# Naming the gathered rows earlier: an edit in VectorE's and GpSimd's order of the expert stage

## The chip, the cores and the metric

The kernel runs on one core of one Trainium2 chip. The metric is the device time of one execution in microseconds (us). In the text PE is TensorE (matrix products and transposes), ACT is ScalarE, DVE is VectorE, POOL is GpSimd and SP is SyncE, which only issues transfers here. Each engine works through its own list of instructions in order. Engines meet through semaphores: an instruction adds to a counter when it has ended, and another engine's list holds at a wait until the counter has the value.

## The reference, cut to what matters

The input is 16 batches of 56 tokens of 512 values, and 16 contexts of 1500 rows of 512 values. A layer of cross attention comes first, then a layer with 16 experts, of which each token uses its best four, and one shared expert that all tokens use:

```python
x = x + xattn(layernorm(x), ctx, Wq, bq, Wk, bk)        # softmax(Q K^T / sqrt(512)) ctx
h = layernorm(x)
scores = sigmoid(h @ gate_w.T) + bias                   # 896 tokens x 16 experts
w, idx = top_k(scores, 4);  w = w / (sum(w) + 1e-20)
out = sum over the four experts e of  w_e * (silu(h Wg_e) * (h Wu_e)) Wd_e
out = out + (silu(h Sg) * (h Su)) Sd
x = x + out
```

## The kernel before, in words

**Stages.** Attention is done in eight turns of two batches, to about 280 us of the trace. The rest is the expert layer. Its tokens are worked in tiles of 128 rows. Tiles 0 to 6 are the 896 tokens in their order, for the shared expert. From tile 7 on (`SHARED` is 7) come the routed tiles: each belongs to one expert and holds up to 128 tokens that chose it. How many there are depends on the data; in this run there are 34, tiles 7 to 40. DVE writes a table (`plan`) that says for each tile which expert it has, which column of the token lists names its rows, how many thirds of the experts' weights have to be split by then, and which tile was the first of its expert. The engines read it into registers, in `entry`.

**One routed tile.** GpSimd fetches its 128 rows from HBM with an indirect DMA into `taken[i]` (`gather`, L439 to L446); the row numbers stand in `take_at[i]`. A row is the 512 normalised values and the token's 16 expert weights. PE turns the rows into columns (bank `b4`, `taken_transpose`), ACT rounds them into `taken_hi`, and DVE writes what the rounding left, `taken_lo` (`taken_to_lo`, L1295). PE then forms the two up products in twelve matrix instructions of 512 columns: high part of the rows by high and low part of the weights (`up_hi`, eight), low part of the rows by the high weights (`up_lo`, four). ACT takes a tanh (`half`), DVE makes from it `gated_rows` and then `z_rows`, into which the token's weight for this expert goes (`silu_rows`; the weight is `taken_w`, one column of the gathered row, copied by `take_weight`, L1307 to L1309). PE turns `z_rows` (`z_transpose`, bank `b5`), ACT rounds (`zt_hi`), DVE writes the rest (`zt_lo`, `z_to_lo`, L1311), and PE forms the down product in six instructions, the last two of which need `zt_lo` (`down`). ACT copies the result into `y_sb[i]` (`keep_y`, L925) and the place of its rows into `add_at[i]` (`name_add`, L930). GpSimd adds the tile into the output with an indirect DMA (`add`, L448 to L461).

**Buffers.** `taken`, `take_at`, `add_at`, `y_sb` and `taken_w` have two places each, which the tiles use in turn. `keep_y` of tile t waits until the add of tile t-2 has landed. An add also waits until all adds of the experts before its own have landed, since the same token's row can be in both.

**Weights.** Experts' weights come from HBM on SP's queue into three places of `w_raw`. ACT rounds them in thirds into `w_hi` (L896), DVE subtracts into `w_lo` (`third_lo`, L1279). Both do so at the end of a step, in `more_thirds`, as many thirds as the plan has due. ACT's part waits until PE has ended the down product before. SP loads a further expert when the thirds of an earlier one have been split.

**Order of a step.** The engines' lists are written out by hand; there is a loop over pairs of steps. In step t:

- PE: `z_transpose(t-1)`, `up_lo(t)`, transposes of tile t+1, `down(t-1)`, wait for the weights, `up_hi(t+1)`.
- ACT: `z_to_hi(t-1)`, `half(t)`, `taken_to_hi(t+1)`, `keep_y(t-2)`, `name_add(t-2)`, `more_thirds(t+1)`.
- DVE: `z_to_lo(t-1)`, `silu_rows(t)`, `taken_to_lo(t+1)`, `take_weight(t+1)`, `name_take(t+3)` (L1302 to L1305), `more_thirds(t+1)`.
- GpSimd, two tiles at a time: `gather(t+5)`, `add(t)`, in this order. The gather waits for `take_named`, which `name_take` of the same tile raises.

So GpSimd's gather of tile T waits for the end of DVE's step T-3, in which ACT also writes the result of tile T-5, whose add stands behind that gather. That the buffer of tile T-2 has been read before the gather overwrites it needs no wait of its own: DVE names tile T after `taken_to_lo(T-2)`, and that follows the transposes.

Of the kernel before, what the change touches and what calls it, by code (L numbers as in the profile page):

```python
# [37 lines left out]
SHARED = TOKENS // P  # L38
# [34 lines left out]
def moe_attention_kernel(nc, x, ctx, ctx_t, wq, bq, wk, bk, gate_t, gate_b, experts, shared,  # L73
# [14 lines left out]
    with es:  # L88
# [3 lines left out]
        def sem(name):  # L92
            return es.enter_context(nc.semaphore(name))
# [32 lines left out]
        with nc.sbuf_tensor("shared_raw", [P, WFREE], fp32) as shared_raw:  # L126
# [125 lines left out]
                              for n in ("b3", "b4", "b5", "b6", "b7"))  # L252
# [24 lines left out]
        gathered, added, shared_taken = ([sem(f"{n}{i}") for i in range(2)] for n in ("gathered", "added", "shared_taken"))  # L277
        take_named, add_named = sem("take_named"), sem("add_named")
        tt_ready, taken_hi_ready, taken_lo_ready, w_ready = (sem(n) for n in ("tt_ready", "taken_hi_ready",
                                                                              "taken_lo_ready", "w_ready"))  # L280
        gu_ready, half_ready, gated_ready, z_rows_ready = (sem(n) for n in ("gu_ready", "half_ready", "gated_ready",
                                                                           "z_rows_ready"))
# [10 lines left out]
        def settle(eng):  # L293
            eng.sem_inc(waited, 1)
# [26 lines left out]
        def entry(eng, table, at, most):  # L321

            return eng.value_load(plan[0:1, bass.ds(at + table, 1)], min_val=0, max_val=most)  # L323

        def inner_pairs(eng):

            return eng.value_load(plan[0:1, T_HALF:T_HALF + 1], min_val=TOKENS * TOPK // P // 2 - 2, max_val=TILES // 2 - 2)
# [81 lines left out]
        @block.gpsimd  # L409
        def _(pool):  # L410
            nc.gpsimd.memset(neg_half[:], -0.5).then_inc(pool_step, 1)
            nc.gpsimd.memset(zero_rows[:], 0.0).then_inc(init_ready, 1)
            pool.wait_ge(pool_step, 1)

            pool.wait_ge(init_ready, 1)

            for i in range(2):
                pool.dma_start(out[TOKENS + i * HALF:TOKENS + (i + 1) * HALF, :], zero_rows[0:HALF, 0:DIM]
                               ).then_inc(added[i], 16)

            def power(i):
                pool.wait_ge(var_ready, i + 1)
                nc.gpsimd.tensor_tensor(rstd[:], var_eps[:], neg_half[:], ALU.pow).then_inc(rstd_ready, 1)  # L423

            power(0)
            power(1)
            with pool.Fori(1, PAIRS - 1) as p:
                power(p * 2)
                power(p * 2 + 1)
            power(2 * PAIRS - 2)  # L430

            def add_shared(t):

                pool.wait_ge(ysb_ready, t + 1)
                nc.gpsimd.indirect_dma_start(
                    out[:, :], bass.IndirectOffsetOnAxis(ap=shared_at[:, t:t + 1], axis=0),
                    y_sb[:, t % 2 * DIM:(t % 2 + 1) * DIM], None, compute_op=ALU.add).then_inc(added[t % 2], 16)


            def gather(t, i):  # L440

                pool.wait_ge(take_named, t - (SHARED - 1))
                settle(pool)
                nc.gpsimd.indirect_dma_start(  # L444
                    taken[i][:, :], None, h_rows[:, :], bass.IndirectOffsetOnAxis(ap=take_at[i][:, 0:1], axis=0)
                    ).then_inc(gathered[i], 16)  # L446

            def add(t, i):  # L448

                first = entry(pool, T_FIRST, t - SHARED, TILES + SHARED)  # L450
                pool.wait_ge(added[0], pool.snap((first + 1) // 2 * 16 + 16, min_val=16, max_val=16 * TILES))
                settle(pool)
                pool.wait_ge(added[1], pool.snap(first // 2 * 16 + 16, min_val=16, max_val=16 * TILES))
                settle(pool)
                pool.wait_ge(add_named, t - (SHARED - 2))
                settle(pool)
                pool.wait_ge(ysb_ready, t + 1)
                settle(pool)
                nc.gpsimd.indirect_dma_start(  # L459
                    out[:, :], bass.IndirectOffsetOnAxis(ap=add_at[i][:, 0:1], axis=0), y_sb[:, i * DIM:(i + 1) * DIM],  # L460
                    None, compute_op=ALU.add).then_inc(added[i], 16)  # L461

            pool.wait_ge(shared_named, 1)
            power(2 * PAIRS - 1)
            pool.wait_ge(acc_stored, 2 * 32)
            add_shared(0)
            add_shared(1)
            add_shared(2)
            add_shared(3)
            pool.wait_ge(init_stored, 16)  # L470
            pool.wait_ge(h_stored, PAIRS * 32 + 16)
            pool.wait_ge(plan_ready, 1)
            n_inner = inner_pairs(pool)
            gather(SHARED, 1)
            gather(SHARED + 1, 0)
            add_shared(4)
            gather(SHARED + 2, 1)
            gather(SHARED + 3, 0)
            add_shared(5)
            gather(SHARED + 4, 1)  # L480
            add_shared(6)
            with pool.Fori(0, n_inner - 1) as pair:
                for k in range(2):
                    t = pair * 2 + (SHARED + k)
                    gather(t + 5, k)
                    add(t, 1 - k)
            t = n_inner * 2 + (SHARED - 2)
            gather(t + 5, 0)
            for k in range(6):
                add(t + k, 1 - k % 2)  # L490
            for i in range(2):
                pool.wait_ge(added[i], n_inner * 16 + 48 + (SHARED + 1 - i) // 2 * 16)
# [519 lines left out]
        def _(dve):  # L1012
# [272 lines left out]
            def more_thirds(t):  # L1285

                upto_t = entry(dve, T_PIECES, t - SHARED, THIRDS * EXPERTS)
                with dve.If_lt(done, upto_t):
                    with dve.Fori(dve.snap(done, min_val=0, max_val=THIRDS * EXPERTS), upto_t) as n:
                        dve.wait_ge(hi_ready, n + 1)  # L1290
                        settle(dve)
                        third_lo(dve.snap(n % (SETS * THIRDS) * THIRD, min_val=0, max_val=(SETS * THIRDS - 1) * THIRD))
                    dve.reg_mov(done, upto_t)

            def taken_to_lo(t):  # L1295
                dve.wait_ge(taken_hi_ready, t + 1)
                settle(dve)
                nc.vector.tensor_tensor(taken_lo[:].rearrange("p k n -> p (k n)"), b4[:, :],  # L1298
                                        taken_hi[:].rearrange("p k n -> p (k n)"), ALU.subtract
                                        ).then_inc(taken_lo_ready, 1)  # L1300

            def name_take(t, i):  # L1302

                col = entry(dve, T_COL, t - SHARED, LISTS + EXPERTS - 1)
                nc.vector.tensor_copy(take_at[i][:], list_at[:, bass.ds(col, 1)]).then_inc(take_named, 1)  # L1305

            def take_weight(t, i):  # L1307
                e = entry(dve, T_EXPERT, t - SHARED, EXPERTS - 1)
                nc.vector.tensor_copy(taken_w[:, i:i + 1], taken[i][:, bass.ds(e + DIM, 1)]).then_inc(w_ready, 1)  # L1309

            def z_to_lo(t):  # L1311
                dve.wait_ge(zt_hi_ready, t + 1)
                settle(dve)
                nc.vector.tensor_tensor(zt_lo_cols[:], b5[:, 0:INNER], zt_hi_cols[:], ALU.subtract  # L1314
                                        ).then_inc(zt_lo_ready, 1)

            def silu_rows(t, i):
                gate_rows(t, i)
                dve.wait_ge(w_ready, t - (SHARED - 1))
                settle(dve)  # L1320
                dve.wait_ge(gated_ready, t + 1)
                settle(dve)
                nc.vector.scalar_tensor_tensor(z_rows[:], gated_rows[:], taken_w[:, i:i + 1], tile_banks[i][:, INNER:], ALU.mult,
                                               ALU.mult).then_inc(z_rows_ready, 1)
# [58 lines left out]
            dve.wait_ge(hi_ready, THIRDS)  # L1383
            third_lo(2 * THIRD)
            n_inner = inner_pairs(dve)
            taken_to_lo(SHARED)
            take_weight(SHARED, 1)
            name_take(SHARED + 2, 1)

            def step(t, i):  # L1390
                z_to_lo(t - 1)
                silu_rows(t, i)
                taken_to_lo(t + 1)
                take_weight(t + 1, 1 - i)
                name_take(t + 3, 1 - i)
                more_thirds(t + 1)

            more_thirds(SHARED)
            step(SHARED, 1)
            with dve.Fori(0, n_inner + 1) as pair:  # L1400
                for k in range(2):
                    step(pair * 2 + (SHARED + 1 + k), k)
            t = n_inner * 2 + (SHARED + 3)
# [67 lines left out]
```

## Time and profile before

| what | us |
|---|---|
| median of 3 runs | 553.05 (546.88 to 556.69) |
| the profiled execution | 548.86 |
| span of its trace | 547.1 |
| attention, from the start | about 280 |
| first routed step to last product of PE | about 321 to 531 |
| PE, DVE, ACT, POOL busy | 490.3, 259.4, 155.4, 110.8 |

The profiled execution's own time is 1.8 us above its span and 4.2 us below the median of the runs. The page's rows have an engine, a line of the kernel, what is written and read, how often, the busy time and the idle time ahead of it with what ended it. "issue" as such a cause means that the engine's sequencer was busy with its own registers and branches, or that the trace shows no other cause. PE's clock stands in tenths or as a share of full speed.

### The profile page before, as it was taken

The page shows a single profiled execution, that of the slowest core. Times are in us where ns is not written, and L with a number is a line of the kernel's source. Part 1 is how long each engine was busy: PE and PEld are TensorE (multiplying, and loading weights), DVE is VectorE, ACT ScalarE, POOL GpSimd, SP SyncE. Part 2 cuts the span into 40 slices and gives each one's busy share as a digit, 9 for nine tenths or more (in the row PEclk, how much of TensorE's full clock was granted, in tenths as well). Part 3 has the DMA queues.
Part 4 walks back from the last instruction along what each step waited for, and adds up shares of the span by engine and source line. Part 5 has one row for each costly group of instructions (what it writes and reads, how often), then busy time and mean ns, then how long its engine had stood idle before and what let it go on. Part 6 is the DMA issues. An engine that isn't in the chain of part 4 may idle for free.

```text
span 547.1 us, 10804 instructions
## 1 busy us (share of the span) xinstructions
PE 490.3 (90%) x2472; PEld 293.8 (54%) x2473; DVE 259.4 (47%) x707; ACT 155.4 (28%) x303; POOL 110.8 (20%) x100
## 2 busy tenths in 40 slices
PE   3999999999999999999899878989898988899970
PEld 1583535353636363543467646767676656577740
DVE  3203337373645445453448874545455646545420
ACT  0000402020203021210222263435363545444430
POOL 1000000000000000000002233444344442444431
PEclk9969999999999999999799989999898999899985
DMA  9999999999999999999646667876749585455552
GB/s 214 399 423 424 388 424 419 411 428 401 427 400 425 400 423 411 417 426 418 241 114 159 157 207 197 270 230 115 195 124 261 98 212 174 80 84 108 97 64 32
DMA packets 28231, 149.04 MB, mean 272 GB/s; under 512 B 4072, under 2 KB 4200, under 8 KB 16424
## 3 DMA queue, kind: packets, MB, share of 16 engines
q1 hardware_dynamic: 15832, 123.08, 56.6%
q0 software_dynamic: 8720, 20.21, 20.2%
q10 hardware_dynamic: 3664, 5.57, 3.3%
q8 instruction: 7, 0.11, 0.1%
q14 instruction: 8, 0.07, 0.0%
HBM read 133.84 MB, written 15.01 MB: 272 GB/s over the span
## 4 chain that ended last, share of the span: by engine, by line
PE 67%; DMA 14%; issue 6%; DVE 4%; ACT 3%; DVEq 2%; ACTq 2%; POOLq 1%; POOL 0%; SPq 0%
PE b L573 16%; PE scores L549 15%; PE b L679 14%; DMA out<-y_sb,add_at 10%; PE b L537 6%; PE b L499 4%; PE scores L679 3%; DMA w_raw<-in_experts 3%; PE scores L511 2%; PE b L563 2%; DMA w_qk<-in_wk 1%; PE b L586 1%; DVEq L323 1%; ACTq L323 1%; ACT w_hi L896 1%
## 5 line engine op out<-in xcount | busy, mean ns | idle before, releaser
L573 PE MATMUL b<-ctx_rows,probs_t 125*64 125x512 f32 (+1 forms) x384 | 86.4, 600 | 0.0
L549 PE MATMUL scores<-ctx_cols,g_t 128*64 128x500 f32 x384 | 84.8, 586 | 0.0
L459 POOL DMA_INDIRECT out<-y_sb,add_at x34 | 54.6, 1605 | 52.2 <-ACT add_at L930 21.8
L423 POOL TENSOR_TENSOR rstd<-var_eps,neg_half 128x1 f32<-128x1 f32 x16 | 8.8, 551 | 268.5 <-DVE var_eps L1021 268.5
L1279 DVE TENSOR_TENSOR w_lo<-w_raw,w_hi (+1 forms) x33 | 39.7, 1223 | 41.2 <-ACT w_hi L896 29.8
L679 PE MATMUL b<-w_hi,taken_hi 128*128 x136 | 57.5, 423 | 1.1 <-ACT taken_hi L907 1.1
L679 PE MATMUL b<-w_lo,taken_hi 128*128 x136 | 55.9, 411 | 0.0
L573 PEld LDWEIGHTS b<-ctx_rows,probs_t 125*64 125x64 f32 (+1 forms) x384 | 26.4, 138 | 48.3 <-issue 47.4
L549 PEld LDWEIGHTS scores<-ctx_cols,g_t 128*64 128x64 f32 x384 | 26.3, 137 | 48.3 <-issue 48.3
L444 POOL DMA_INDIRECT taken<-h_rows,take_at x34 | 34.1, 1002 | 76.4 <-DVE take_at L1305 74.7
L896 ACT CAST w_hi<-w_raw (+1 forms) x33 | 33.8, 1048 | 31.3 <-issue 15.1
L679 PE MATMUL b<-w_hi,taken_lo 128*128 x136 | 40.0, 416 | 0.0
L1052 DVE TENSOR_REDUCE row_max<-scores 128x1 f32<-128x1500 f32 x8 | 13.8, 1721 | 47.2 <-PE scores L549 47.2
L835 ACT COPY h_t_now<-b 128x512 f32<-128x512 f32 x7 | 4.1, 586 | 109.4 <-PE b L499 109.4
L537 PE MATMUL b<-xn_t,w_fold 128*128 128x128 f32 x256 | 33.1, 291 | 1.4 <-ACT xn_t L819 1.4
L679 PEld LDWEIGHTS b<-w_hi,taken_hi 128*128 128x128 f32 x136 | 27.3, 200 | 13.0 <-issue 7.1
L537 PEld LDWEIGHTS b<-xn_t,w_fold 128*128 128x128 f32 x256 | 31.7, 205 | 2.1 <-issue 1.1
L917 ACT CAST zt_hi<-b 128x256 fp32r<-128x256 f32 x41 | 15.2, 371 | 54.7 <-PE b L702 54.6
L1314 DVE TENSOR_TENSOR zt_lo<-b,zt_hi 128x256 fp32r<-128x256 f32 x41 | 17.2, 421 | 28.2 <-ACT zt_hi L917 26.0
L679 PEld LDWEIGHTS b<-w_lo,taken_hi 128*128 128x128 f32 x136 | 27.2, 200 | 5.6
L907 ACT CAST taken_hi<-b 128x512 fp32r<-128x512 f32 x41 | 24.1, 587 | 16.4 <-PE b L499 14.9
L1298 DVE TENSOR_TENSOR taken_lo<-b,taken_hi 128x512 fp32r<-128x512 f32 x41 | 28.1, 684 | 1.4 <-ACT taken_hi L907 1.3
(213 smaller groups left out, 682.0 us busy)
## 6 DMA issues: line engine op xcount, KB each, us to landing
ctx_rows<-in_ctx SPq DMA_DIRECT2D x48, 1024.0 KB, 15.0
ctx_cols<-in_ctx_t SPq DMA_DIRECT2D x32, 1500.0 KB, 17.8
w_raw<-in_experts SPq DMA_DIRECT2D x11, 1536.0 KB
h_rows<-h ACTq DMA_DIRECT2D x16, 115.5 KB
taken<-h_rows SPq DMA_DIRECT2D x7, 264.0 KB
out<-xs ACTq DMA_DIRECT2D x2, 784.0 KB
shared_raw<-in_shared SPq DMA_DIRECT2D x1, 1536.0 KB, 32.3
xs<-in_x ACTq DMA_DIRECT2D x12, 112.0 KB
```

Of the source, the lines that this page charges most:

```text
L444: nc.gpsimd.indirect_dma_start(taken[i][:, :], None, h_rows[:, :], bass.IndirectOffsetOnAxis(ap=take_at[i][:, 0:1], axis=0)).then_inc(gath ...
L459: nc.gpsimd.indirect_dma_start(out[:, :], bass.IndirectOffsetOnAxis(ap=add_at[i][:, 0:1], axis=0), y_sb[:, i * DIM:(i + 1) * DIM], None, c ...
L499: last = nc.tensor.transpose(bank[:, k * P:(k + 1) * P], src[:, k * P:(k + 1) * P], ident)
L537: last = nc.tensor.matmul(b7[:, m * P:(m + 1) * P], w_fold[:, k, m * P:(m + 1) * P], xn_t[:, k, :], start=(k == 0), stop=(k == KD - 1))
L549: last = nc.tensor.matmul(scores[HALF * b:HALF * (b + 1), n, 0:CHUNK], g_t[:, k, HALF * b:HALF * (b + 1)], ctx_cols[:, at:at + CHUNK], sta ...
L573: last = nc.tensor.matmul(b3[HALF * b:HALF * (b + 1), :], probs_t[0:rows_in(p), at:at + HALF], ctx_rows[0:rows_in(p), g, b, c * DIM:(c + 1 ...
L679: return nc.tensor.matmul(bank, a[:, k, :], w[:, bass.ds(at + k * n, n)], start=start, stop=stop)
L896: nc.scalar.copy(w_hi[:, bass.ds(at, THIRD)], w_raw[:, bass.ds(at, THIRD)]).then_inc(hi_ready, 1)
L907: nc.scalar.copy(taken_hi[:].rearrange("p k n -> p (k n)"), b4[:, :]).then_inc(taken_hi_ready, 1)
L1279: nc.vector.tensor_tensor(w_lo[:, bass.ds(at, THIRD)], w_raw[:, bass.ds(at, THIRD)], w_hi[:, bass.ds(at, THIRD)], ALU.subtract).then_inc(l ...
L1298: nc.vector.tensor_tensor(taken_lo[:].rearrange("p k n -> p (k n)"), b4[:, :], taken_hi[:].rearrange("p k n -> p (k n)"), ALU.subtract).th ...
L1314: nc.vector.tensor_tensor(zt_lo_cols[:], b5[:, 0:INNER], zt_hi_cols[:], ALU.subtract).then_inc(zt_lo_ready, 1)
```

## The change

Three edits. DVE's step now begins with `take_weight(t+1)` and `name_take(t+3)`, which stood behind `taken_to_lo(t+1)`; in the stretch ahead of the loop they also move ahead of `taken_to_lo(7)`. `take_weight` has two new waits: for the gather of its own tile, and for the `z_rows` of tile t-2 (which used the same place of `taken_w`; its argument t there is the tile whose weight is taken). `gather` of tile t has a new wait, until the rows of tile t-2 have been transposed. `settle` is the register-free increment that the kernel puts behind each wait.

```diff
@@ gather(t, i), GpSimd
                 pool.wait_ge(take_named, t - (SHARED - 1))
                 settle(pool)
+                pool.wait_ge(tt_ready, t - 1)
+                settle(pool)
                 nc.gpsimd.indirect_dma_start(
@@ take_weight(t, i), VectorE
             def take_weight(t, i):
+                dve.wait_ge(gathered[i], (t - SHARED) // 2 * 16 + 16)
+                settle(dve)
+                dve.wait_ge(z_rows_ready, t - 1)
+                settle(dve)
                 e = entry(dve, T_EXPERT, t - SHARED, EXPERTS - 1)
                 nc.vector.tensor_copy(taken_w[:, i:i + 1], taken[i][:, bass.ds(e + DIM, 1)]).then_inc(w_ready, 1)
@@ VectorE's list
             n_inner = inner_pairs(dve)
-            taken_to_lo(SHARED)
             take_weight(SHARED, 1)
             name_take(SHARED + 2, 1)
+            taken_to_lo(SHARED)
 
             def step(t, i):
+                take_weight(t + 1, 1 - i)
+                name_take(t + 3, 1 - i)
                 z_to_lo(t - 1)
                 silu_rows(t, i)
                 taken_to_lo(t + 1)
-                take_weight(t + 1, 1 - i)
-                name_take(t + 3, 1 - i)
                 more_thirds(t + 1)
```

## Rows read from the trace of the kernel before

**Rows 1.** The page: the chain that ended last, by engine.
```profile
PE 67%; DMA 14%; issue 6%; DVE 4%; ACT 3%; DVEq 2%; ACTq 2%; POOLq 1%; POOL 0%; SPq 0%
```

**Rows 2.** Waits, 330 to 547 us: engine and what waited, releaser, us, times, longest.
```profile
POOL taken L444 <- DVE take_at L1305: 69.5, 27, 6.6
...
DVE w_lo L1279 <- ACT w_hi L896: 27.9, 13, 4.2
...
ACT y_sb L925 <- DMA out<-y_sb,add_at: 22.1, 10, 4.7
...
DVE w_lo L1279 <- issue: 11.4, 8, 1.9
```

**Rows 3.** Timeline of POOL: start, us, engine, line, operation [idle before, releaser].
```profile
437.25 1.58 POOL L459 DMA_INDIRECT out<-y_sb,add_at  x1 [2.18 <-ACT add_at L930]
439.98 0.98 POOL L444 DMA_INDIRECT taken<-h_rows,take_at  x1 [1.15 <-DVE take_at L1305]
441.91 1.58 POOL L459 DMA_INDIRECT out<-y_sb,add_at  x1 [0.95 <-issue]
```

**Rows 4.** Timeline of ACT around the same tiles.
```profile
436.94 0.19 ACT L930 COPY add_at<-list_to 128x1 int32 x1
...
445.26 0.59 ACT L925 COPY y_sb<-b 128x512 f32<-128x512 f32 x1 [3.12 <-DMA out<-y_sb,add_at]
```

**Rows 5.** The chain of waits: start, length, link.
```profile
437.25 7.82 DMA out<-y_sb,add_at
```

**Rows 6.** Timeline of DVE, one step and the next one's head.
```profile
435.05 1.22 DVE L1279 TENSOR_TENSOR w_lo<-w_raw,w_hi  x1 [1.80 <-issue]
...
437.48 0.68 DVE L1298 TENSOR_TENSOR taken_lo<-b,taken_hi 128x512 fp32r<-128x512 f32 x1
438.14 0.15 DVE L1309 COPY taken_w<-taken 128x1 f32 x1
438.97 0.15 DVE L1305 COPY take_at<-list_at 128x1 int32 x1 [0.68 <-issue]
440.26 1.23 DVE L1279 TENSOR_TENSOR w_lo<-w_raw,w_hi  x1 [1.14 <-issue]
441.40 0.42 DVE L1314 TENSOR_TENSOR zt_lo<-b,zt_hi 128x256 fp32r<-128x256 f32 x1
```

**Rows 7.** Timeline of PE in that step: transposes, then the products that need `zt_lo`.
```profile
435.12 0.63 PE L499 MATMUL b<-cst,taken 128*128 128x128 f32 x4 [0.31 <-issue]
...
442.47 0.63 PE L679 MATMUL scores<-w_hi,zt_lo 128*128 x2
```

**Rows 8.** Timeline of DVE two steps on.
```profile
448.51 1.22 DVE L1279 TENSOR_TENSOR w_lo<-w_raw,w_hi  x1 [4.16 <-ACT w_hi L896]
449.66 0.42 DVE L1314 TENSOR_TENSOR zt_lo<-b,zt_hi 128x256 fp32r<-128x256 f32 x1
```

**Rows 9.** Timeline of PE: the product that needs `zt_lo` after it.
```profile
450.22 0.71 PE L679 MATMUL b<-w_hi,zt_lo 128*128 x2
```

**Rows 10.** Timeline of PE: its idle times behind a late result copy.
```profile
363.13 0.49 PE L679 MATMUL b<-w_hi,zt_hi 128*128 x1 [1.34 <-ACT zt_hi L917]
...
393.01 0.69 PE L679 MATMUL scores<-w_hi,zt_hi 128*128 x1 [2.39 <-ACT zt_hi L917]
...
449.02 0.49 PE L679 MATMUL b<-w_hi,zt_hi 128*128 x1 [2.48 <-ACT zt_hi L917]
...
469.58 0.50 PE L679 MATMUL scores<-w_hi,zt_hi 128*128 x1 [1.82 <-ACT zt_hi L917]
```

**Rows 11.** A stretch of 4 us: PE busy, granted clock, DMA share, GB/s.
```profile
392.00:396.00 4.00, 2.99 (x7) 0.64 0.49 69
```

**Rows 12.** Timeline of PE: the first routed step's down product.
```profile
328.52 0.70 PE L679 MATMUL b<-shared_hi,zt_lo 128*128 128x512 f32 x2 [0.71 <-DVE zt_lo L1314]
```

**Rows 13.** Timeline of POOL: the last gather.
```profile
513.89 0.98 POOL L444 DMA_INDIRECT taken<-h_rows,take_at  x1 [2.77 <-DVE take_at L1305]
```

**Rows 14.** Timeline of POOL: a longer add.
```profile
411.14 2.33 POOL L459 DMA_INDIRECT out<-y_sb,add_at  x1 [0.94 <-issue]
```

## The prediction

> **What bounds the kernel now.** I read the page's chain first: it is PE for 67%, and the second link is DMA with 14%, nearly all of it the adds into the output [rows 1]. So the routed part is PE's work with holes in it, and some holes hang on an add. The list of waits of that part, read next, says who holds whom. GpSimd waits 69.5 us in 27 times for the name of the next gather, and ACT waits 22.1 us in 10 times for an add to land before it may copy the next result [rows 2]. The timeline ties the two together. The result and add place of one tile are ready at 437.13 (436.94 and 0.19) [rows 4], but its add is issued at 441.91, behind a gather that began at 439.98, after a name that DVE finished at 439.12 [rows 3, 6]. That is a lag of 4.8 us, and walking the timelines I found 4 us or more in 22 of the 34 tiles. An add that is 4.8 us late lands late, and the copy two tiles on waits for it: 3.12 us at 445.26, for the add of 437.25, which took 7.82 us to land [rows 4, 5]. ACT is in order, so rounding of weights and of `zt_hi` slip too, and PE stands for 2.48 us [rows 10]. Four holes of PE come about so, 1.34, 2.39, 2.48 and 1.82 us, 8.0 in all [rows 10].
>
> A second bound lies on DVE. Where a weight third is split, `zt_lo` comes right behind it. At 449.66 + 0.42 = 450.08 it ends and PE's product begins 0.14 later [rows 8, 9]: PE has no slack. At 441.40 + 0.42 = 441.82 PE has 0.65 to spare [rows 6, 7]. There are 21 such steps (13 in which the third waited for ACT, 8 in which DVE's sequencer was the last [rows 2]); walking them one by one, PE starts within 0.2 us of `zt_lo` in 12.
>
> **The change, part by part.**
>
> *Earlier names, earlier gathers.* The name of a gather was finished 0.98 us after `taken_to_lo` (438.14 to 439.12) [rows 6]; now it comes behind the last third of the step before. In the step shown the third of the step before began at 435.05; with the copies gone from in front of it, it begins 0.98 sooner and ends near 435.3, and the name is written near 436.3 [rows 6]. The new wait, for the transposes of tile T-2, ends at 435.12 + 0.63 = 435.75 [rows 7], sooner than the name; so I price it at nothing there. Name to gather takes 439.98 - 439.12 = 0.86, gather 0.98, to the add 0.95 [rows 3, 6]: 436.3 + 2.8 = 439.1 in place of 441.91. Adds come about 2.8 us sooner where only the gather holds them; where an add waits for its predecessor's landing the gain is handed down that chain, less than whole. I take 1.9. Behind the gather's wait on GpSimd stands only the add, and ACT waits for that.
>
> *Gain at PE's holes.* A copy that waits 1.9 less shortens its hole by as much, or closes it: 1.34 + 1.9 + 1.9 + 1.82 = 7.0 [rows 10]. Bounds: 3 (the chain of landings keeps its 7.82 us [rows 5]) to 8.0.
>
> *Clock.* Behind the hole of 2.39 us the granted clock was 0.64 of 2.4 GHz in the next 4 us, a product taking 0.69; behind that of 2.48 the product took 0.49, at the full clock [rows 10, 11]. A fall costs about 4 x 0.36 = 1.5 us. I count one as saved, 1.5; bounds 0 and 3 (two).
>
> *End.* The last gather waits 2.77 us for its name, at 513.89 [rows 13], and the last six adds come behind it. They are spaced by results and landings, so of the 2.8 only about 0.9 arrives; bounds 0 and 2.
>
> *The copies on the way to `zt_lo`.* This is the cost. The two copies and the table read between them are 0.15 + 0.68 + 0.15 = 0.98 [rows 6]. Before, they lay in front of the third, which mostly waited for ACT anyway, so they cost nothing there. Now they lie between the third and `zt_lo`. The first copy's own table read and two waits can run while the third does (1.23), as it runs now behind the 0.68 of `taken_lo`, with no idle time in the row; I price them at nothing there. In the 8 steps in which the sequencer was last, the third starts up to 0.98 sooner in turn, and `zt_lo` stays: 0.3 us for all 8. In the 13 others: in five the third started a third of a microsecond behind ACT's cast and PE had 0.15 to spare, 5 x (0.98 - 0.15) = 4.2 (448.51 is one, [rows 8, 9]). One had 0.69, cost 0.3. Three had 0.15, but their third can start 0.5 sooner, 3 x 0.35 = 1.0. Four have slack enough. Together 5.8. The first routed step has it too, behind its burst of thirds [rows 12]: 0.8. Sum 6.6. Bounds: 1.5, if both table reads hide, and 15: at 435.05 the third began 1.80 behind the name with nothing to wait for, where 1.14 is usual [rows 6], so a sequencer that takes longer over its branches adds 0.5 or more and the push can be 1.5 instead of 0.98, in all 21 steps.
>
> *Steps without a third, and the wait for the gather.* There `zt_lo` waits for ACT, and PE has 1.0 or more to spare; the two copies fit in. The list of waits has no row of anyone who waits for a gather's landing (its longest are in [rows 2]), and the weight is asked for two steps after its gather: nothing. The wait for `z_rows` is for DVE's own earlier work: nothing.
>
> *Ports.* An add issued at 411.14, while DVE split thirds, took 2.33 us where others take 1.58 [rows 14, 3]; earlier adds will lie beside a third more often. At 0.75 on GpSimd it stays off the path. The Trainium skill (SBUF — State Buffer, "SBUF: two separate sides") has a rule here: VectorE with two SBUF inputs and GpSimd take a shared port pair in turns, the later one blocked for the whole instruction. By it a `w_lo` could wait behind an add's descriptors; no row here has a `w_lo` above 1.23 us.
>
> **Sum.** Gains 7.0 + 1.5 + 0.9 = 9.4, losses 6.6: -2.8. The profiled execution's 548.86 becomes 546.1. It lies 4.2 under the median of its runs, so against 553.05 I say 550.3, rounded 550. Two per cent is 11 us, and the three runs themselves lie 9.8 apart: about what this can tell from no change.
>
> **Rivals.**
>
> *Adds rule (faster), 0.22.* All of the holes and both clock falls go, and the push hides: 8 + 3 + 2 - 1.5 = 11.5 less at most, 8 in the middle: 545. For it: 69.5 us of GpSimd's waits are for the name. Against: 12 of 21 steps leave `zt_lo` no slack.
>
> *`zt_lo` rules (slower), 0.20.* The push is 1.5 in every step with a third, because the moved table read and waits come behind a branch of the loop. Loss 12 to 15, gain 5: +8, 561. It decides from a push of about 1.2 us on. For it: 1.80 against 1.14 [rows 6]. Against: a delayed PE delays the next need as well, so consecutive steps share one push.
>
> *The port, 0.04.* The third waits for the add's descriptors, 1.58 - 0.8 on average in half of the 21 steps, 8 us on `zt_lo`'s path, less the 2.8: 558. This is what the rule of the Trainium skill on the shared port pair would make of the earlier adds.
>
> *The gather doesn't move, 0.06.* If the transposes or the adds' landings let it go at its old time, only the loss stays: +6.6, 560. Against: the transposes ended 3.4 us before the name.
>
> *Forecast, 0.48.* Both effects, nearly even: 546 to 556.
>
> **How the numbers follow.** The range adds to 546 to 556 the middle of both main rivals: 543 to 561. Faster by over 2% (below 542) needs the best end of the first rival, 0.09. Slower (above 564) needs the worst of the second or two together, 0.11. Within, 0.80.
>
> **What would show it.** The time from `add_at` to its add falls from 4.8 to about 2; GpSimd's wait for `take_at` falls well below 69.5; ACT's wait for landings falls from 22.1 to under 10. `take_at` then stands behind `w_lo`, and `zt_lo` starts 1.0 behind the third's end instead of at it; PE's waits for `zt_lo` come into the list with some 6 us. Wrong I would be if lag falls and ACT's wait doesn't (landings rule), or if the distance from third to `zt_lo` is 1.5 or more.

## The result, and the profile after

| kernel | median us | runs |
|---|---|---|
| before | 554.23 | 4 (546.88 to 556.69) |
| changed | 562.56 | 4 (561.37 to 564.59) |

The ratio of changed to before is 1.019, 95% interval 1.0138 to 1.0243: slower by 1.4 to 2.4%. The medians lie 8.3 us apart. Some executions of a kernel fall into a slower state and take one or two per cent longer, so the ratio leaves them out, and so do the times of the experiments below. A repeat (e5) gave 1.0216 (1.0151 to 1.028). The forecast was 550 with a range of 543 to 561, so it was wrong in sign and the time lies outside the range. What came nearest is the rival called "`zt_lo` rules", at 561. The traced execution of the changed kernel has a span of 559.6 us, 12.5 more than before.

The waits of the routed part, 330 to 560 us, after (columns as in [rows 2]):

```profile
POOL taken L446 <- DVE take_at L1307: 38.6, 11, 6.0
DVE w_lo L1281 <- ACT w_hi L898: 36.7, 21, 4.5
POOL taken L446 <- issue: 33.3, 12, 4.2
...
POOL taken L446 <- PE b L501: 15.2, 8, 2.9
ACT w_hi L898 <- PE scores L681: 13.8, 9, 2.8
PE b L681 <- DVE zt_lo L1320: 13.1, 12, 1.6
ACT w_hi L898 <- PE b L681: 11.9, 7, 2.9
PE scores L681 <- DVE zt_lo L1320: 8.5, 8, 2.0
...
ACT y_sb L927 <- DMA out<-y_sb,add_at: 7.3, 3, 4.7
```

Both effects of the forecast are there: adds come sooner, and `zt_lo` comes later. The first can't be read from GpSimd's wait for names, though its row fell from 69.5 us [rows 2] to 38.6. A gather now ends with two waits, and where the second had long been met the wait stands under "issue" (33.3 us): e11 below, with the names at their old places, has a row of 38.9 as well. All idle time ahead of the gathers is 38.6 + 33.3 + 15.2 = 87.1 us where it was 71.2 (69.5 and 1.7 of issue). What shows the earlier adds is their lag behind the result, 4.2 us on average before and 2.5 after, and ACT's wait for landed adds, 22.1 before and 7.3 after.

The 15.2 us are gathers whose names stood and whose transposes did not. One of the eight (POOL, then PE):

```profile
486.42 0.98 POOL L446 DMA_INDIRECT taken<-h_rows,take_at  x1 [2.94 <-PE b L501]
```
```profile
484.96 0.60 PE L501 MATMUL b<-cst,taken 128*128 128x128 f32 x4
```

Its name was finished at 483.24, the transposes at 485.56.

On the other side PE now waits 13.1 + 8.5 = 21.6 us for `zt_lo`, in 20 places; before, that wait was 2.7 us in 3 places. ACT's weight casts wait 25.7 us for PE's down products in 16 places, 10.5 in 8 before. And all 21 groups of thirds (the thirds that are split in one step) wait for ACT's cast, where 8 had been held by the sequencer [rows 2].

DVE after, two steps in a row, to be held against [rows 6]:

```profile
441.60 1.23 DVE L1281 TENSOR_TENSOR w_lo<-w_raw,w_hi  x1 [1.16 <-ACT w_hi L898]
443.07 0.15 DVE L1315 COPY taken_w<-taken 128x1 f32 x1 [0.25 <-issue]
443.90 0.15 DVE L1307 COPY take_at<-list_at 128x1 int32 x1 [0.68 <-issue]
444.05 0.42 DVE L1320 TENSOR_TENSOR zt_lo<-b,zt_hi 128x256 fp32r<-128x256 f32 x1
...
447.59 1.23 DVE L1281 TENSOR_TENSOR w_lo<-w_raw,w_hi  x1 [1.56 <-ACT w_hi L898]
449.55 0.15 DVE L1315 COPY taken_w<-taken 128x1 f32 x1 [0.74 <-issue]
450.73 0.15 DVE L1307 COPY take_at<-list_at 128x1 int32 x1 [1.03 <-issue]
450.88 0.42 DVE L1320 TENSOR_TENSOR zt_lo<-b,zt_hi 128x256 fp32r<-128x256 f32 x1
```

The first third ends at 442.83 and `zt_lo` starts 1.22 later; the second ends at 448.82 and `zt_lo` starts 2.06 later. Before, `zt_lo` started 0.09 before the third's stated end (440.26 + 1.23 against 441.40 [rows 6]). I call this the distance. Worked out so for all 21 groups of thirds, its mean is -0.09 us before and 1.62 after. PE at the second place:

```profile
450.15 0.39 PE L681 MATMUL scores<-w_lo,zt_hi 128*128 x1
451.45 0.71 PE L681 MATMUL scores<-w_hi,zt_lo 128*128 x2 [0.92 <-DVE zt_lo L1320]
```

It stands for 0.92 us and starts 0.15 after `zt_lo` ends (451.30), as in [rows 8, 9]. Behind some of these stops the granted clock falls. This is the stretch around one of 1.50 us at 419.65. Columns: stretch, length, then busy us (and count) of PE, PEld, DVE, ACT and POOL, then clock, DMA share, GB/s:

```profile
416.00:420.00 4.00, 1.96 (x9) 1.23 (x8) 3.16 (x7) 1.86 (x6) 0.00 (x0) 0.92 0.73 166
420.00:424.00 4.00, 4.00 (x14) 3.08 (x14) 1.37 (x4) 0.04 (x1) 2.56 (x2) 0.66 0.61 206
```

PE did 1.96 us of work in the first 4 us and its granted clock was 0.66 over the next, a mean between its levels of 1.2 and 2.4 GHz: the products there took 0.63 us at first and 0.39 from 422.77 on. Another stop of 1.50 us, at 471.6, had no such fall behind it (1.00 from 472 to 476). The whole routed part after and, below it, before:

```profile
330.00:560.00 230.00, 186.47 (x798) 132.05 (x796) 104.51 (x225) 94.22 (x196) 88.65 (x67) 0.93 0.60 139
```
```profile
330.00:547.00 217.00, 182.63 (x794) 131.15 (x792) 101.72 (x225) 93.82 (x196) 88.16 (x67) 0.94 0.63 148
```

Of the 13 us that it grew, 3.8 are busy time of PE, whose mean clock is 0.93 where it was 0.94 (and whose trace has four more products), and 9.2 are PE's idle time (43.5 against 34.4).

### The profile page after: what moved, and what is told of

Read it like the earlier page. It is cut to its first block, busy times and chain, and to the rows that moved or that the text cites. A ratio compares the mean times of both kernels' runs of the same rounds, so it can differ in the third digit from the quotient of the medians.

```text
span 559.6 us, 10934 instructions
## 1 busy us (share of the span) xinstructions
PE 493.6 (88%) x2472; PEld 294.7 (53%) x2473; DVE 261.4 (47%) x707; ACT 156.0 (28%) x303; POOL 110.7 (20%) x100
## 4 chain that ended last, share of the span: by engine, by line
PE 62%; DMA 8%; issue 8%; DVEq 6%; ACT 5%; DVE 4%; ACTq 3%; SPq 0%; POOL 0%; POOLq 0%
PE scores L551 15%; PE b L575 14%; PE b L681 13%; PE b L539 6%; DVEq L323 4%; DMA w_raw<-in_experts 4%; ACT w_hi L898 3%; PE b L501 3%; PE scores L513 2%; ACTq L323 2%; PE b L565 2%; DMA out<-y_sb,add_at 2%; DVE zt_lo L1320 2%; PE scores L681 1%; DMA w_qk<-in_wk 1%
## 5 line engine op out<-in xcount | busy, mean ns | idle before, releaser
L681 PE MATMUL b<-w_hi,taken_hi 128*128 x136 | 59.4, 437 | 1.2 <-ACT taken_hi L909 1.1
L1281 DVE TENSOR_TENSOR w_lo<-w_raw,w_hi (+1 forms) x33 | 39.7, 1223 | 38.9 <-ACT w_hi L898 38.9
L919 ACT CAST zt_hi<-b 128x256 fp32r<-128x256 f32 x41 | 15.2, 371 | 67.6 <-PE b L704 67.2
L501 PE MATMUL b<-cst,taken 128*128 128x128 f32 x164 | 25.4, 278 | 4.3 <-DMA taken<-h_rows,take_at 2.5
```

The source lines that it names most:

```text
L501: last = nc.tensor.transpose(bank[:, k * P:(k + 1) * P], src[:, k * P:(k + 1) * P], ident)
L681: return nc.tensor.matmul(bank, a[:, k, :], w[:, bass.ds(at + k * n, n)], start=start, stop=stop)
L1281: nc.vector.tensor_tensor(w_lo[:, bass.ds(at, THIRD)], w_raw[:, bass.ds(at, THIRD)], w_hi[:, bass.ds(at, THIRD)], ALU.subtract).then_inc(l ...
```

## The experiments

Each is given as a change to the kernel before or to the changed one. Times are medians. Ratios are to the kernel before, run on the same chip; they are estimated from the single runs and differ from the quotients of the medians by up to 0.007. e1 to e4 ran on one chip, e5 to e11 on a second, e12 on a third, so kernels of different chips are compared by their ratios. "Distance" is from the third's end to `zt_lo`'s start, mean of 21. It and the two waits (us) are from one traced execution each. The last column is ACT's wait for landed adds.

| run | what | us | before | ratio (95%) | distance | PE waits for zt_lo | ACT waits for adds |
|---|---|---|---|---|---|---|---|
| e1 | changed, late gather | 559.07 | 549.19 | 1.018 (medians of 2 and 13 runs, no interval) | 1.41 | 14.6 | 13.4 |
| e2 | copies behind silu_rows | 560.26 | 549.19 | 1.0147 (1.0072, 1.0223) | -0.08 | 1.7 | 21.0 |
| e3 | before, add ahead of gather | 545.29 | 549.19 | 0.9928 (0.9884, 0.9971) | -0.08 | 2.5 | 5.8 |
| e4 | changed, reads ahead | 541.96 | 549.19 | 0.9857 (0.9812, 0.9901) | 0.13 | 3.2 | 10.3 |
| e5 | changed again | 563.15 | 550.59 | 1.0216 (1.0151, 1.028) | 1.65 | 20.5 | 6.6 |
| e6 | e4, late gather | 548.13 | 550.59 | 0.996 (0.9935, 0.9986) | 0.13 | 3.5 | 21.2 |
| e7 | e4, add ahead of gather | 548.87 | 550.59 | 0.9959 (0.9921, 0.9997) | 0.47 | 3.4 | 5.6 |
| e8 | changed, loop of four steps | 560.72 | 550.59 | 1.0176 (1.0103, 1.0249) | 1.50 | 21.5 | 6.3 |
| e9 | changed, copies twice | 603.72 | 552.23 | 1.0907 (1.0826, 1.0987) | 3.25 | 49.3 | 3.9 |
| e10 | e4, one read ahead | 547.51 | 552.23 | 0.9869 (0.9781, 0.9956) | 0.75 | 8.5 | 11.4 |
| e11 | before, new wait of GpSimd | 556.38 | 552.23 | 1.0077 (1.0034, 1.0121) | -0.09 | 2.8 | 34.4 |
| e12 | e4, copies behind z_to_lo | 543.38 | 551.02 | 0.9794 (0.9719, 0.987) | -0.04 | 2.9 | 10.0 |

The theory after the result: the loss is the distance between third and `zt_lo`, made above all by the table reads; the earlier adds are worth something by themselves.

**e1_push_only: the push without the earlier gathers.**

```diff
                 pool.wait_ge(tt_ready, t - 1)
                 settle(pool)
+                pool.wait_ge(taken_lo_ready, t - 1)
+                settle(pool)
```

> The changed kernel, but a gather of tile T also waits until VectorE has written taken_lo of tile T-2, so gathers and adds go at about their old times while the copies stay at the head of the step. Theory zt_lo (the copies and table reads between the last third and zt_lo stop PE): the loss stays whole and the gain of earlier adds is gone, so slower than the changed kernel's 562.6 by 3 to 8 us, 566 to 570; ACT's wait for landings back from 7 to about 20 us, PE's wait for zt_lo still about 20 us. Rival gather (earlier gathers and adds hurt, by the port or the DMA rings): the time falls back to 554 to 557.

1.018 of the kernel before, the changed kernel's own ratio and not above it. The rival falls: with late gathers the time does not come back to that of the kernel before. But the theory's number is missed too: ACT's wait rose from 7.3 to 13.4 us and the time did not. So while the push on `zt_lo` stands, no worth of earlier adds can be seen. It rests on two runs, and PE's wait for `zt_lo` is also lower here (14.6 us, 21.6 in the changed kernel), so a loss of the adds may hide behind it.

**e2_behind_silu: the copies elsewhere, reads still open.**

```diff
             def step(t, i):
-                take_weight(t + 1, 1 - i)
-                name_take(t + 3, 1 - i)
                 z_to_lo(t - 1)
                 silu_rows(t, i)
+                take_weight(t + 1, 1 - i)
+                name_take(t + 3, 1 - i)
                 taken_to_lo(t + 1)
```

> The changed kernel with the two copies moved from the head of the step to behind silu_rows, ahead of taken_to_lo; waits as changed. Theory zt_lo: nothing lies between a third and zt_lo any more, PE's wait for zt_lo falls from 21 to under 5 us, names come about 0.7 us sooner than in the kernel before, so adds are a little earlier: 549 to 555, at or a little under the kernel before. Rival gather: the new waits of GpSimd and the earlier gathers keep it at 558 to 563.

PE's wait for `zt_lo` is down to 1.7 us, as expected, and the time is not: 560.26. The theory fell short here. Its DVE:

```profile
445.74 0.48 DVE L1329 SCALAR_TENSOR_TENSOR z_rows<-gated_rows,taken_w,b 128x256 f32<-128x256 f32 x1
446.95 0.15 DVE L1315 COPY taken_w<-taken 128x1 f32 x1 [0.73 <-issue]
447.78 0.15 DVE L1307 COPY take_at<-list_at 128x1 int32 x1 [0.68 <-issue]
448.00 0.69 DVE L1300 TENSOR_TENSOR taken_lo<-b,taken_hi 128x512 fp32r<-128x512 f32 x1
```

The copy comes 0.73 us after `z_rows` has ended, and the second read takes 0.68 more, so `taken_lo` comes 1.78 us behind `z_rows`. In the kernel before it came right after it, as it still does in the changed one. `taken_lo` ends at 448.69 and PE's `up_lo` begins at 448.99. PE's following transposes are late for their sequencer in 30 places:

```profile
PE b L501 <- issue: 9.0, 30, 0.6
```

Before, this row was 1.4 us in 4. So the reads still cost where they are open. But that is not all of e2's loss. In the traces the result of tile 10 is 5.7 us later than in the kernel before and that of the last tile 12.6: the first part arises in the first routed steps, as in e11, whose new wait of GpSimd e2 has too. And ACT's wait for landings is 21.0, so nothing is won by earlier adds.

**e3_add_first: the adds alone.**

```diff
-                    gather(t + 5, k)
                     add(t, 1 - k)
+                    gather(t + 5, k)
```

> The kernel before with one edit: in GpSimd's loop the add of tile t is issued ahead of the gather of tile t+5. VectorE's order is the old one. Theory zt_lo with an add gain: adds come within 1 to 2 us of their result where no landing holds them, ACT's wait for landings falls from 22 to under 8 us, PE has no push on zt_lo, so faster than before by 4 to 9 us, 545 to 550. Rival landings (adds are bound by one another's landing, so freeing them brings nothing) : 553 to 556, ACT's wait stays above 15. Rival late gathers: a gather behind an add that waits for a landing comes too late for PE's transposes, 556 or more, with PE waiting for DMA.

545.29, ratio 0.9928, in the sense of the theory though its interval reaches 0.9971. ACT's wait fell to 5.8 us. Part of the gain went to the other rival: PE waits for gathers that come too late.

```profile
PE b L499 <- DMA taken<-h_rows,take_at: 8.9, 7, 2.5
```

**e4_reads_ahead: the table reads out of the open stretch.**

```diff
+            def read_ahead(t):
+                dve.reg_mov(next_e, entry(dve, T_EXPERT, t + 1 - SHARED, EXPERTS - 1))
+                dve.reg_mov(next_col, entry(dve, T_COL, t + 3 - SHARED, LISTS + EXPERTS - 1))
             def step(t, i):
-                take_weight(t + 1, 1 - i)
-                name_take(t + 3, 1 - i)
+                copies(t + 1, 1 - i)        # same waits and copies, from the registers
                 z_to_lo(t - 1)
                 silu_rows(t, i)
                 taken_to_lo(t + 1)
+                read_ahead(t + 1)
                 more_thirds(t + 1)
```

> The changed kernel, but the two table reads of the copies are done at the end of the step before, ahead of the thirds, and kept in registers; waits and copies stay at the head. Theory zt_lo: the distance from the last third to zt_lo falls from 1.3 and 2.1 us (every other step) to 0.4 to 1.0, PE's wait for zt_lo from 21 to about 8 us, 552 to 557. Rival copies (the copies themselves and their new semaphore waits, not the table reads, make the distance): no change, 561 to 564.

541.96: better than the theory had it by 10 us. The waits and the copies are all still at the head of the step, and the distance is about 0.04 in 14 of the 21 groups and up to 0.36 in the others. One of the others:

```profile
450.35 1.22 DVE L1281 TENSOR_TENSOR w_lo<-w_raw,w_hi  x1 [1.90 <-issue]
451.59 0.15 DVE L1408 COPY taken_w<-taken 128x1 f32 x1
451.72 0.15 DVE L1410 COPY take_at<-list_at 128x1 int32 x1
451.87 0.42 DVE L1320 TENSOR_TENSOR zt_lo<-b,zt_hi 128x256 fp32r<-128x256 f32 x1
```

So the loss needs the reads: without them the new waits of DVE and the copies fit beside the third. What the waits add while the reads stand open no run shows by itself.

Part of the gain is clock. From 330 to 518 us no stretch of 4 us is below full clock in e4's trace; the kernel before has falls to 0.64, 0.70 and 0.62 (from 392, 412 and 472), the changed one to 0.72, 0.66, 0.60 and 0.64 (from 400, 420, 480 and 512).

**e5_after_again.** 

> The changed kernel itself, as the measure for the others of this call on the same chip. Theory and rivals alike: 558 to 565 against 549 to 554 of the kernel before, PE's wait for zt_lo about 20 us.

As expected: 563.15, and 20.5 us of waiting for `zt_lo`.

**e6_reads_late_gather: e4 with e1's wait.** The edit is that of e1.

> The kernel of e4_reads_ahead (short push on zt_lo), with the gather held back until taken_lo of tile T-2 is written, so adds go at about their old times. Theory two terms (early adds are worth several us by themselves): 545 to 550, 3 to 8 us above e4, ACT's wait for landings back to 15 us or more. Rival reads (e4 is fast only because the table reads left the open stretch, and the adds' times are worth nothing): 541 to 543, as e4.

548.13, ratio 0.996 against e4's 0.9857: the intervals lie apart. Without the push, the earlier gathers and adds are worth about 6 us (0.0103 of 550); ACT's wait is back at 21.2.

**e7_reads_add_first: e4 with e3's edit.**

> The kernel of e4_reads_ahead with the add of tile t issued ahead of the gather of tile t+5. Theory two terms: adds are 1 to 2 us earlier again where no landing holds them, ACT's wait for landings under 6 us: 536 to 541. Rival late gathers: behind an add that waits for a landing the gather comes late, and VectorE, which now waits for it at the head of the step, carries that to zt_lo: 542 to 550, with DVE or PE waiting for the gather's DMA.

The rival is right: 548.87. ACT's wait is the lowest of the fast kernels (5.6), but both DVE and PE wait for late gathers:

```profile
DVE taken_w L1408 <- DMA taken<-h_rows,take_at: 14.4, 7, 3.8
PE b L501 <- DMA taken<-h_rows,take_at: 12.3, 8, 4.1
```

**e8_four_steps: is the longer distance the loop's turn?**

```diff
-            with dve.Fori(0, n_inner + 1) as pair:
-                for k in range(2):
-                    step(pair * 2 + (SHARED + 1 + k), k)
+            with dve.Fori(0, 8) as four:
+                for k in range(4):
+                    step(four * 4 + (SHARED + 1 + k), k % 2)
```

> The changed kernel with VectorE's loop body made four steps long, turned 8 times instead of 16. Theory loop (the longer distance from third to zt_lo, 2.1 instead of 1.3 us, is the loop's turn in front of the exposed table reads): only every fourth step has the long distance, PE's wait for zt_lo falls by about 4 us, 557 to 560 where the changed kernel has 562. Rival parity (odd and even steps differ for another reason): every second step keeps 2.1 us, no change of time.

560.72, ratio 1.0176, an interval that overlaps the changed kernel's: no gain of time is shown, and PE's wait for `zt_lo` did not fall (21.5 us, 20.5 in e5). The number of steps in the loop is also fixed here, which the kernel reads from its data otherwise. But the distances did what the theory of the loop says. In e5 seven groups have 2.18 to 2.39 us, each in a step behind the loop's turn (an eighth there has 1.34). In e8 four have 2.09 to 2.46, each again behind a turn; the three that no longer stand behind one have 1.24, 1.40 and 1.78 (and the eighth 0.86). Such a step in the changed kernel, and the same step in e8, where the loop no longer turns:

```profile
397.12 0.15 DVE L1315 COPY taken_w<-taken 128x1 f32 x1 [1.37 <-issue]
```
```profile
399.02 0.15 DVE L1315 COPY taken_w<-taken 128x1 f32 x1 [0.27 <-issue]
```

So the loop's turn lengthens the idle time before the first copy, mostly from 0.25 to 0.73 us. What stretches the second read, from 0.68 to as much as 1.41, stays open: it is long in some steps of both kinds.

**e9_twice: double the cost.** Two more reads and copies into a spare tile behind the two.

> The changed kernel with two further table reads and one-column copies (into a spare tile nobody reads) behind the two at the head of the step. Theory zt_lo: the distance from third to zt_lo grows by 2 x (0.68 + 0.15) = 1.7 us, from 1.6 to about 3.3 on average, in 21 steps, less what following steps share: 12 to 30 us slower than the changed kernel, 575 to 593. Rival DVE isn't the path (the loss came from elsewhere): under 5 us.

603.72, more than forecast. The distance came as worked out (3.25), and PE's wait for `zt_lo` is 49.3 us. I had counted the 21 steps with a third and left out the others. They have no room for 1.7 us more either, but they explain little: 4.5 us of that wait, in seven of them. In the steps with a third it rose from 21 to 44.8. The clock fell as well, to a mean of 0.91 from 330 to 530 us (0.97 in the changed kernel). How the 40 us are made up of these is not shown.

**e10_half_ahead: one read left open (the weight's).**

> The kernel of e4_reads_ahead, but only the name's table read is done ahead; the weight's stays at the head of the step. Theory zt_lo: one read of 0.68 us is exposed in part (the third runs 1.23 us beside it), distance 0.5 to 0.9 us, time about half way or nearer to e4: 546 to 553. Rival (any read at the head stops the run-ahead alike): 558 to 563.

Distance 0.75, ratio 0.9869, not to be told from e4. The open read makes 0.62 us of distance (0.75 against 0.13) and 5.3 us more waiting of PE than in e4 (8.5 against 3.2), and little or no time. The name's read on top of it, which is e5, makes 0.90 us more distance, 12.0 more waiting and 19 us (0.9869 to 1.0216). So time is not in proportion to distance: nearly nothing at 0.75, 19 us at 1.65.

**e11_wait_only: GpSimd's new wait alone.**

```diff
                 pool.wait_ge(take_named, t - (SHARED - 1))
                 settle(pool)
+                pool.wait_ge(tt_ready, t - 1)
+                settle(pool)
```

> The kernel before with GpSimd's new wait for the transposes alone. The name comes later than the transposes, so all theories expect no change, 548 to 554; a rise of 3 us or more would be the cost of a wait on GpSimd's queue.

The expectation of nothing is wrong: 1.0077 (1.0034 to 1.0121), about 4 us. The name was there at 446.37 and the gather began at 447.39, 1.02 later. The median of all 34 is 1.00, before it was 0.84. DVE, then POOL:

```profile
446.22 0.15 DVE L1307 COPY take_at<-list_at 128x1 int32 x1 [0.68 <-issue]
```
```profile
447.39 0.98 POOL L446 DMA_INDIRECT taken<-h_rows,take_at  x1 [1.32 <-issue]
449.43 1.58 POOL L461 DMA_INDIRECT out<-y_sb,add_at  x1 [1.06 <-issue]
```

Each add comes 0.25 us later on average (4.45 against 4.2 behind its result), and ACT's wait for landings rises to 34.4 us. It would be natural to lay the 4 us to this small delay in each step, but the traces speak against it. The result copies of tile 10 and of the last tile, before and, below, in e11:

```profile
358.69 0.59 ACT L925 COPY y_sb<-b 128x512 f32<-128x512 f32 x1 [1.34 <-DMA out<-y_sb,add_at]
...
533.35 0.59 ACT L925 COPY y_sb<-b 128x512 f32<-128x512 f32 x1 [4.72 <-DMA out<-y_sb,add_at]
```
```profile
366.00 0.58 ACT L927 COPY y_sb<-b 128x512 f32<-128x512 f32 x1 [4.96 <-DMA out<-y_sb,add_at]
...
540.05 0.58 ACT L927 COPY y_sb<-b 128x512 f32<-128x512 f32 x1 [4.60 <-DMA out<-y_sb,add_at]
```

At tile 7's result e11 is 0.9 us behind, at tile 10's 7.3, at the last 6.7. So the 30 steps in between, nearly all with the new wait, lost nothing. What was lost was lost between tiles 7 and 10. There e11's chain of waits (columns as in [rows 5]) has, one behind the other, an add of a shared tile and two of routed tiles:

```profile
339.65 9.33 DMA out<-y_sb,shared_at
...
350.77 7.02 DMA out<-y_sb,add_at
...
358.93 6.88 DMA out<-y_sb,add_at
```

How the new wait leads to this start, and whether it does in every run, is open: there is one trace. e2, which has the wait too, lost 5.7 us by tile 10; the changed kernel lost 2.2.

The waits for the gather show how such a row is to be read:

```profile
POOL taken L446 <- DVE take_at L1307: 38.9, 15, 6.6
...
POOL taken L446 <- issue: 28.2, 16, 4.8
```

Together that is 67.1 us, where it was 71.2 in the kernel before.

**e12_reads_behind_zt: the best of both.** e4 with `z_to_lo(t - 1)` ahead of the copies.

> The kernel of e4_reads_ahead with the two copies behind z_to_lo instead of ahead of it. Theory zt_lo: the distance from third to zt_lo is -0.09 as in the kernel before, PE's wait for zt_lo under 2 us, names 0.4 to 0.6 us later than in e4, ACT's wait for landings 10 to 13 us: ratio to before 0.98 to 0.99, as e4 within its interval. Rival (the copies' place matters still, on the way to gated_rows): ratio above 0.995.

543.38 against 551.02, ratio 0.9794 (0.9719 to 0.987); the medians give 0.986. PE's wait for `zt_lo` is 2.9 us, where under 2 was expected. With e4 (0.9857) the intervals overlap, so neither place is shown to be better; both beat both kernels.

## Why the prediction was wrong

*The bound it read was right, and worth less than it looked.* GpSimd's lag behind a result is 2.5 us on average (add's start less the later end of `y_sb` and `add_at`, 34 tiles) where it was 4.2, and 22 lags of 4 us or more became 2. ACT's wait for landings fell to 7.3, as forecast under 10. The sign that the prediction set for GpSimd, a wait for `take_at` well below 69.5, proves nothing, since the new wait splits that row (e11).

*The step that failed* is "the copies on the way to `zt_lo`". It took 0.98 us for the two copies and one read, and priced the first copy's read and the two waits at nothing, because they "can run while the third does". That was put at 6.6 us. Measured, the distance rose from -0.09 to 1.62, by 1.71 us. The first copy's read and the waits do not fit beside the third: DVE is idle for 0.43 us on average before the first copy, which was priced at nothing. The second read leaves 0.90 on average, which was priced at 0.68. The 1.5 us that the prediction had kept as the worst push is below this mean. e4 against e5 prices the step: 0.9857 and 1.0216 of the kernel before, about 20 us, with the place of the reads as the only difference. The bound of the loss was 15.

The row that the zero came from was a different case. There the first read ran behind one `taken_lo` of 0.68 us with nothing to wait for. A third that waits for ACT holds DVE's list until the cast has ended, so the loop's end, the two waits and the read can begin only then. Where DVE was ahead of its work the read was indeed free, as here behind three thirds in a row:

```profile
414.59 3.50 DVE L1281 TENSOR_TENSOR w_lo<-w_raw,w_hi  x3 [1.15 <-ACT w_hi L898]
418.11 0.15 DVE L1315 COPY taken_w<-taken 128x1 f32 x1
418.94 0.15 DVE L1307 COPY take_at<-list_at 128x1 int32 x1 [0.68 <-issue]
```

From the third's end to `zt_lo` (419.08) it is 0.99 us, just the push of the prediction. That the waiting list is the reason elsewhere is my reading of these rows; the prices do not depend on it.

*A second error in the same step* is how it counted. In 8 steps the third was to start 0.98 sooner and save all; in the rival "consecutive steps share one push". The trace is better told as a ring: `zt_lo` late, so the down product ends late, so ACT's cast of the next third starts late, so the third and the next `zt_lo` are late again. ACT's casts wait for PE 10.5 us before, 13.5 in e4, 19.0 in e10, 25.7 and 21.8 in the two traces of the changed kernel and 47.9 in e9. No run cuts the ring by itself, so it is argued, not shown. That all 21 thirds wait for ACT is no proof of it: they do in e10 too, which is fast, since the copies no longer stand before the third.

*The gains were mispriced by being added.* Holes, clock and end stood at 9.4 us. Without the push the early gathers give 6 (e4 against e6). With it no gain is seen (e5 against e1, two runs): ACT, less held by landings, waits for PE. The clock did not get better either: up to 520 us it fell four times, at other places, where it had fallen three times.

*The new wait of GpSimd* was priced at nothing, since the transposes end before the name. In the old order that is so, and still e11 costs about 4 us, in the first routed steps by its trace. In the changed order the margin was small by the prediction's own numbers, 436.3 against 435.75, and in 8 gathers the transposes ended after the name (15.2 us of idle time, the row above). What that costs in time was not measured.

*Ports.* No `w_lo` of the changed kernel is longer than 1.23 us (27 in the routed part, 1.217 to 1.228). Nor did one start late: in all 21 groups the first third starts 0.33 or 0.34 us after ACT's cast has ended, with GpSimd at work beside it or not. So nothing speaks for the port rival here; and e4, with adds as early, is fast. Some adds took longer than 1.58, up to 2.46 us, as one had before (2.33 [rows 14]). The section of the Trainium skill that the prediction cites (SBUF — State Buffer, "SBUF: two separate sides") limits the rule on two SBUF inputs to GpSimd instructions that read SBUF, a condition that the prediction left out.

*The rival that came nearest* had named its point, a push of about 1.2 us, and e10 (0.84 more than before, fast) and e5 (1.74, slow) lie on its two sides. That its 561 was so near to 562.56 is in part luck. It had a loss of 12 to 15 and a gain of 5; measured are about 20 and, with the push, no gain that can be seen. Its reason, the branch of the loop, explains the longest third of the distances (e8) and not the rest. Its best evidence, the table reads' 0.68 and 1.80 against 1.14 [rows 6], was in the rows, and the forecast took the low end of a range whose high end the nearest row with nothing to wait for had shown.

## What to carry to other kernels

In this kernel a table read into a register left DVE idle for 0.68 us or more between two copies, 0.90 on average. A copy of 0.15 us that needs such a read is cheap only where its engine is ahead of its data, as behind the 0.68 us of `taken_lo` [rows 6] or the three thirds above. So when a small step is moved to the head, look at what its register reads and waits stand behind, and read into registers ahead of the last long wait. Before adding gains and losses, see whether both act on one ring: here the gain was seen only with the loss gone. And when an edit adds a wait, add up all rows of the instruction behind it before you say that a wait fell.

## What the hardware showed unexpectedly

One more wait and its count on GpSimd's list lengthened the way from a name to its gather by 0.16 us (0.84 to 1.00 in the median); the steps from tile 10 on lost nothing by it in e11's trace, and yet the kernel took about 4 us more, by its trace in the first routed steps. Four one-column copies with their reads instead of two (0.15 us of work each) cost about 40 us over 33 steps (603.72 against 563). Two copies whose registers were filled beforehand moved `zt_lo` by only 0.13 us (distance 0.04 instead of -0.09, in 14 of 21 groups of e4). In the changed kernel the first third of a group started 0.33 or 0.34 us after ACT's cast in all 21 groups, whether GpSimd was at work or not.
